# A gated cross-attention and MoLE feed-forward layer: the 26 last context rows in 32x32 tiles, and a new order around scores and values

## The reference, cut to what matters

```python
q = (layernorm(x) @ Wq.T + bq) * D ** -0.5      # x: (4, 1024, 256), 16 heads of D = 16
k, v = ctx @ Wk.T + bk, ctx @ Wv.T + bv         # ctx: (4, 154, 256)
k, q = xpos_apply(k, True), xpos_apply(q, False)        # rotation by position
attn = softmax(q @ k.T) @ v                     # per head, over the 154 context rows
x = x + tanh(g_xattn) * (attn @ Wo.T + bo)
h = relu(mole(layernorm(x), W1, b1, A1, B1, R1))        # 256 -> 1024, with 3 routed LoRA experts
x = x + tanh(g_ffn) * mole(h, W2, b2, A2, B2, R2)       # 1024 -> 256
```

## Time and profile before

| | us |
|---|---|
| median of 3 runs | 584.95 |
| lowest, highest | 583.15, 585.03 |
| the profiled execution, its own time | 584.23 |
| its span (first to last instruction) | 582.4 |
| TensorE busy in the span | 522.7 |
| VectorE busy | 402.3 |
| ScalarE busy | 245.5 |
| GpSimd busy | 84.8 |

### The profile page before, as it was taken

One profiled execution on the slowest core, in us unless ns is written; L12 is line 12 of the kernel. 1 busy time (PEld: TensorE's weight loads), 2 busy tenths in 40 slices (PEclk: granted clock), 3 DMA queues, 4 the chain that ended last, 5 costly groups with the idle time before them and its releaser, 6 DMA issues.

```text
span 582.4 us, 8570 instructions
## 1 busy us (share of the span) xinstructions
PE 522.7 (90%) x3384; PEld 399.7 (69%) x3384; DVE 402.3 (69%) x920; ACT 245.5 (42%) x405; POOL 84.8 (15%) x121
## 2 busy tenths in 40 slices
PE   2668865999999899999999899999999999999897
PEld 1545454864988488855987488856987498748687
DVE  4658465866889568958889478958888487925533
ACT  3152614364353616453364616454355526251330
POOL 2418012010020112011110112011100120010000
PEclk9965986999999999999999999999999999999898
DMA  8301010010100110010101010111002000100001
GB/s 273 98 21 37 1 37 2 0 51 1 37 1 38 37 38 2 38 49 0 38 1 57 19 37 2 38 48 32 7 1 75 0 1 2 41 35 1 1 36 37
DMA packets 6131, 18.49 MB, mean 32 GB/s; under 512 B 932, under 2 KB 1772, under 8 KB 5964
## 3 DMA queue, kind: packets, MB, share of 16 engines
q10 hardware_dynamic: 4005, 12.53, 6.2%
q1 hardware_dynamic: 2087, 5.42, 2.8%
HBM read 13.49 MB, written 4.19 MB: 30 GB/s over the span
## 4 chain that ended last, share of the span: by engine, by line
PE 68%; DVE 15%; ACT 10%; POOL 3%; issue 3%; DMA 1%; ACTq 0%; DVEq 0%; POOLq 0%
PE psF L1084 11%; PE psF L1145 10%; PE psX L1128 5%; DVE max_t L748 5%; PE psX L1199 4%; PE psX L995 4%; PE psX L1013 4%; ACT probs L536 4%; PE psO L1213 3%; ACT xn L426 3%; PE psF L1213 3%; PE psF L1216 3%; PE psO L1216 3%; PE psX L1115 3%; DVE ln_s L589 2%
## 5 line engine op out<-in xcount | busy, mean ns | idle before, releaser
L748 DVE TENSOR_REDUCE max_t<-psX 128x4 fp32r<-128x616 f32 x128 | 99.4, 795 | 5.1 <-PE psX L1128 2.1
L536 ACT ACTIVATE probs<-psX 128x1024 f32<-128x1024 f32 x64 | 64.0, 1024 | 50.9 <-PE psX L1199 50.9
L1145 PE MATMUL psF<-w_hi,h_hi 128*128 128x284 f32 (+1 forms) x240 | 72.7, 303 | 0.0
L1145 PE MATMUL psF<-w_lo,h_hi 128*128 128x284 f32 (+1 forms) x240 | 70.8, 295 | 0.0
L1145 PE MATMUL psF<-w_hi,h_lo 128*128 128x284 f32 (+1 forms) x240 | 70.7, 295 | 0.0
L1128 PE MATMUL psX<-km,qT 96*128 96x308 f32 x256 | 63.5, 335 | 5.7 <-DVE max_t L748 5.0
L1128 PEld LDWEIGHTS psX<-km,qT 96*128 96x128 f32 x256 | 47.9, 200 | 20.8 <-DVE max_t L748 12.4
L446 ACT ACTIVATE h_hi<-psF 128x512 fp32r<-128x512 f32 x59 | 34.4, 594 | 56.1 <-PE psF L1090 56.0
L326 POOL TENSOR_TENSOR x<-x,tab 128x256 f32<-128x256 f32 x32 | 22.3, 727 | 195.6 <-DMA x<-in_x_dram 195.6
L1145 PEld LDWEIGHTS psF<-w_hi,h_hi 128*128 128x128 f32 x240 | 45.7, 190 | 4.8 <-issue 4.6
L1084 PE MATMUL psF<-xT_lo,w_hi 128*128 128x512 f32 x118 | 47.0, 402 | 0.0
(11 more groups left out here) (187 smaller groups left out, 1044.2 us busy)
## 6 DMA issues: line engine op xcount, KB each, us to landing
x<-in_x_dram ACTq DMA_DIRECT2D x8, 512.0 KB, 3.4
x_ln<-in_x_dram ACTq DMA_DIRECT2D x7, 512.0 KB, 3.3
out_dram<-x ACTq DMA_DIRECT2D x7, 512.0 KB, 2.6
heads_t<-in_w_dram SPq DMA_DIRECT2D x1, 1024.0 KB, 8.2
heads_t<-in_w_dram SPq DMA_DIRECT2D x1, 994.0 KB, 4.8
tab<-in_tables_dram SPq DMA_DIRECT2D x1, 674.0 KB, 6.7
x_ln<-in_x_dram SPq DMA_DIRECT2D x1, 512.0 KB, 3.3
wkv_sb<-in_wkv_dram SPq DMA_DIRECT2D x1, 512.0 KB, 9.3
```

What stands on the lines that cost most here:

```text
L536: nc.scalar.activation(dst, psX[:, 2 * (i % 2):2 * (i % 2) + 2, :], ACT.Exp).then_inc(sc_exp.sem, 1)
L748: V.tensor_reduce(max_t[:, k, half, :].rearrange("p (h g) -> p g h", h=2)[:, 2 * j:2 * j + 2, :], psX[:, 2 * j:2 * j + 2, 0:2 * S].rearran ...
L1145: ins = mm(out_bank(d, k)[:, cs], a[:, m, tokens(k)], w[:, m, cs], start=m == 0 and i == 0, stop=m == HT - 1 and i == 2)
```

## The change

The rest of the values no longer runs as a 128x128 block-diagonal product. `vr_sb` shrinks to 32 columns, and each head's rest is a product of its own of 32 rows and 32 columns (`values_rest`); heads that sit on the same 32 rows of `probs_r` (j) write the same bank: `pv_bank(j)` is psO for even j and psF 2 for odd j. A half (`half`) covers two values of j, that is eight heads. The main values go by `part`: four parts of four heads each, in the two banks. The order of heads in `wo` on the host follows. In the score stage, the second "rest" becomes score 3 (it was 5), main pairs come in the order 0, 2, 4, 6, 1, 3, 5, 7, and the places on TensorE become: values part 0 after score 3; context transposes after score 5; values part 1, the first half of the rest and `project_k` after score 7; then scores 8 and 9, the second half of the rest, parts 2 and 3, and after all of them the queries. `rotate_keys` is cut in two: the biases (`keys_bias`) stay in the score stage, the rotation and splitting move to the head of the next step on VectorE. Keys are transposed after output tile 1 and not before output tile 0, and `project_v` stands between the two tiles. In the last step, output tiles 0, 1, 2 take the places of 2, 0, 1.

```diff
-        vr_sb = sb("vr_sb", [P, NQ, P])
+        vr_sb = sb("vr_sb", [P, NQ, 32])
-            return psF[:, g // 2, :] if g % 2 else psO[:, :]
+            return psF[:, 2, :] if j % 2 else psO[:, :]
@@ score order
-                if i % 5 == 0:
-                    pe.wait_ge(max_rows[i // 5].sem, max_rows[i // 5].at(c))
+                if i in (0, 3):
+                    pe.wait_ge(max_rows[i // 3].sem, max_rows[i // 3].at(c))
@@ values
-                mm(pv_bank(g), vr_sb[:, g, :], probs_r[:, g, :], start=True, stop=False)
-                for j in range(4):
-                    h = 4 * g + j
-                    ins = mm(pv_bank(g)[32 * j:32 * j + 32, :], v_sb[:, h, :], probs[:, h % 8, :], start=False, stop=True)
+                half = part // 2
+                for q in (2 * (part % 2), 2 * (part % 2) + 1):
+                    for j in (2 * half, 2 * half + 1):
+                        ins = mm(tile_of(j, q), v_sb[:, 4 * q + j, :], probs[:, 2 * q + j % 2, :],
+                                 start=half == 0, stop=half == 1)
+            def values_rest(c, half):
+                if half:
+                    pe.wait_ge(pv_t.sem, pv_t.at(c, 2))
+                for q in range(4):
+                    for j in (2 * half, 2 * half + 1):
+                        rows = slice(32 * j, 32 * j + 32)
+                        ins = mm(tile_of(j, q), vr_sb[rows, q, :], probs_r[rows, q, :], start=half == 1, stop=half == 0)
+                if not half:
+                    ins.then_inc(pv_ps.sem, 1)
@@ VectorE, end of a step
                 head_blocks(c, 1)
+                if u == 1 and not last:
+                    keys_bias(b + 1)
                 head_norm(c, 0)
                 head_back(c, 0)
-                if u == 1 and not last:
-                    rotate_keys(b + 1)
+                head_low(c, 0)
                 head_blocks(c, 2)
-                head_low(c, 0)
+                head_blocks(c, 3)
+                head_norm(c, 1)
+                head_back(c, 1)
+                head_low(c, 1)
                 if not last:
                     q_bias(c + 1)
@@ tables
-SCORE_STEPS = [("rest", 0), ("main", 0), ("main", 2), ("main", 4), ("main", 6),
-               ("rest", 2), ("main", 8), ("main", 10), ("main", 12), ("main", 14)]
+SCORE_STEPS = [("rest", 0), ("main", 0), ("main", 2), ("rest", 2), ("main", 4), ("main", 6),
+               ("main", 1), ("main", 3), ("main", 5), ("main", 7)]
```

More of the change, by code:

```diff
@@ L538, in step @@
                         xT_high(c + 1)
-                    if i == 4 and not last and u == 1:
+                    if i == 5 and not last and u == 1:
                         ctx_copy(b + 1)
@@ L759, in gates2 @@
             def gates2(d, pr):
-                dve.wait_ge(g2_c.sem, g2_c.at(d, 3 if d is LAST - 1 and pr == 0 else 2 * pr + 2))
+                dve.wait_ge(g2_c.sem, g2_c.at(d, 2 * pr + 2))
                 K = slice(2 * pr, 2 * pr + 2)
@@ L817, in step @@
                     q_bias(c)
[L818 to L822, removed]
+                    keys_bias(b)
+                if u == 0:
                     rotate_keys(b)
                 q_sine(c, u)
-                if not first:
-                    head_low(d, 1)
                 q_sum(c)
@@ L922, in _ @@
             gates2(e, 0)
+            copy_z2(e, 2)
             copy_z2(e, 3)
@@ L1198, in scores, with tile_of, values @@
                     else:
-                        ins = mm(o_ps, km[:, n // 2, j, 0:P], qT[:, n // 2, :], start=True, stop=True)
+                        ins = mm(o_ps, km[:, n, j, 0:P], qT[:, n, :], start=True, stop=True)
                 ins.then_inc(sc_ps.sem, 1)
-            def values(c, g, first, last):
-                pe.wait_ge(sc_exp.sem, sc_exp.at(c, PV_AFTER[g]))
-                if g == 0:
+            def tile_of(j, q):
+                col = (q + 2 * (j % 2)) % 4
+                return pv_bank(j)[32 * col:32 * col + 32, :]
+            def values(c, part, first):
+                pe.wait_ge(sc_exp.sem, sc_exp.at(c, (3, 6, 8, 10)[part]))
+                if part == 0:
                     pe.wait_ge(maxT_s[1].sem, maxT_s[1].at(c))
@@ L1226, in step @@
                     project_k(b)
-                if u == 0:
-                    if not first:
-                        pe.wait_ge(pv_t.sem, pv_t.at(d, 3))
                     key_transposes(b)
@@ L1295, in step @@
                         transpose_x(c + 1, psF, ln1_out, xT_ps)
-                    if i == 3 and u == 1 and not last:
+                    if i == 3:
+                        values(c, 0, first)
+                    if i == 5 and u == 1 and not last:
                         ctx_transposed(b + 1, ctx_sb)
-                    if i == 6 and u == 1 and not last:
-                        project_k(b + 1)
-                    if last and i in (1, 6, 9):
+                    if i == 7:
+                        values(c, 1, first)
+                        values_rest(c, 0)
+                        if u == 1 and not last:
+                            project_k(b + 1)
+                    if last and i in (1, 5, 9):
                         if i == 1:
@@ L1303, in step @@
                             pe.wait_ge(w1_lo_s.sem, w1_lo_s.at(d))
-                        out_tile(LAST - 1, 2, *{1: (0, 3), 6: (3, 5), 9: (5, 8)}[i])
-                    if i in PV_SLOT:
-                        values(c, PV_SLOT[i], first, last)
+                        out_tile(LAST - 1, 0, *{1: (0, 3), 5: (3, 5), 9: (5, 8)}[i])
+                values_rest(c, 1)
+                values(c, 2, first)
+                values(c, 3, first)
                 if not last:
@@ L1309, in step @@
                     project_q(c + 1, False)
-                values(c, 3, first, last)
             pe.wait_ge(const_v.sem, 1)
@@ L1411 @@
     wkv = _np.concatenate([i["L0_xattn_Wk"].T[:, perm], i["L0_xattn_Wv"].T], 1)
-    wo = i["L0_xattn_Wo"].T.reshape(2, 2, 4, D, E).transpose(2, 1, 3, 0, 4).reshape(P, -1)
+    heads = [4 * ((col + 2 * g) % 4) + 2 * f + g for col in range(4) for g in range(2) for f in range(2)]
+    wo = i["L0_xattn_Wo"].T.reshape(H, D, E)[heads].reshape(4, 2, 2, D, E).transpose(0, 1, 3, 2, 4).reshape(P, -1)
     w1 = i["L0_ffn_W1"].reshape(FT, P, HID).transpose(1, 0, 2).reshape(P, -1)
```

68 lines of the change are left out of this document (35 added, 33 removed).

## The result

| | before | after |
|---|---|---|
| median of 4 runs each, same chip | 584.05 us | 592.45 us |
| lowest and highest | 582.86 to 585.03 | 589.24 to 592.63 |
| ratio, 95% interval | | 1.0132 [1.009, 1.0174] |
| profiled execution, its span | 584.23, 582.4 | 592.31, 590.5 |
| mean granted clock in it | 0.953 | 0.944 |

The prediction said 580.3 us, with a range of 576.5 to 588.0. The time lies above the range and on the other side of no change.

The account below looks back on a forecast made before the run. TensorE, with 68% of the chain, was taken to bound the kernel, along with step heads hanging on VectorE. The terms -3.6 + 3.15 - 1.35 - 2.2 = -4.0 us took 584.23 to 580.3, range 576.5 to 588.

Parts of the forecast that it names:

- Part 1: Score stage: each half of the rest in 32x32 tiles takes TensorE 1.05 us, saving 2.1 us a step.
- Rival 2: In `values_rest`, row tiles take turns: a half costs 2.0 us, 15.2 us on top, 595.5 us; chance 0.13.
- Part 2: Score 3 waits for the maxima rows, 2.3 us after their DMA issue; this eats half the tiles' saving.
- Part 3: Score stage walked: T comes sooner by 0.95 us (step 2), 1.45 (step 3), 2.15 (step 0), 2.7 (last step).
- Part 4: VectorE's work at a step's head: bias ends at T + 3.1; statistics 0.45 us sooner or 1.05 later.
- T: Moment when the score stage's last group ends and output tiles begin, 210.2 us in step 2 before the change.
- u = 1: After steps 1, 3, 5: keys' rotation behind T makes the statistics 1.05 us later, three times, +3.15 us.
- u = 0: After steps 2, 4, 6: statistics about 0.45 us sooner, three times, -1.35 us.
- Step 0's head: After step 0: heads and bias done at 80.05 for 83.86, statistics about 86.2 for 89.80, -3.6 us.
- rival 3: At step 1's head the clock may stay at 2.4 GHz, up to 3 us more, 577.5 us; chance 0.12.
- the end: After the last step: `project_out` starts at 530.2 for 532.43, -2.2 us.
- Rival 1: The middle eats the gain: rows 0.3 us later or VectorE's line 0.5 longer; 582 to 586 us, chance 0.17.

Follow-up runs that it names:

- e7: Changed kernel with the second row of maxima used one score later: 589.17 us, ratio 1.0111.
- e1: Changed kernel with GpSimd's cosine product cut to two heads of one token tile in every step but the first: 576.87 us, ratio 0.9894.
- e2: Kernel before, with GpSimd's cosine waiting until VectorE has turned the second half of the heads back: 592.67 us, ratio 1.0166.
- e8: Changed kernel; after u = 1 the cosine runs beside the values' bias, sine and sum behind the statistics; after u = 0 cosine on VectorE: 595.0 us.
- e12: Changed kernel with GpSimd's cosine cut into four instructions, one for each token tile: 596.33 us in one run.
- e6: Changed kernel with the cosine on VectorE ahead of the sine, none on GpSimd: 588.13 us, median of nine, ratio 1.003.
- e11: Changed kernel with cosine on VectorE, second maxima row one score later, half of output tile 2 ahead of the routes' transposes: 581.11 us, ratio 0.9967.
- e9: Changed kernel with the edits of e8 and e7 together: 591.02 us, ratio 1.0125.
- e5: Changed kernel with half of output tile 2 ahead of the routes' transposes on TensorE: 588.43 us, ratio 1.0121.

## Why the prediction was wrong, point by point

- **Part 1, the rest at 1.05 us a half: right.** 1.02 measured (the prediction's other estimate was 1.03), and two row groups that write psO and psF 2 cost nothing more. Rival 2 (row tiles take turns, 2.0) is out. The row that 1.05 leans on, L1034, has 16 instructions of 256 columns, not 512; it serves because its four tiles stream 1024 columns each, as those of L1216 do, and as the tiles of a half now do in 1.02 us.
- **Part 2, the rows: right in kind, 0.3 us short.** TensorE waits 1.41 to 1.47 us for them in steps 2 to 6 (forecast 1) and starts score 3 at 2.59 after the issue, for the forecast 2.3; the 0.15 for the semaphore stood on no row. e7 prices the wait at 0.7 to 1.0 us a step.
- **Part 3, stage lengths: right.** 190.70 to 210.39 is 19.7 us (forecast 19.6) and 252.55 to 273.84 is 21.3 (21.2). The 0.3 of part 2 hardly shows in them.
- **Part 4, the failed step.** "Sine 1.3" and "T + 3.1 + 3.5" for the rotation took VectorE's durations from rows in which GpSimd was idle, though the same part had just moved GpSimd's cosine to T + 3.1, exactly onto them. I used the cosine's row for its start and not for what would run beside it. The price: after u = 1 the statistics start at T + 18.07 for 16.1, three times 2.0; after u = 0 at T + 11.51 for 10.75, three times 0.8. The second is less than 2.2, because I had put the queries' sum at T + 6.9, where the terms I gave add up to 3.1 + 1.3 + 1.15 = 5.6; that error of 1.3 hid a part.
- **Step 0's head: right, without rival 3.** TensorE's idle time before `project_out` fell from 4.71 to 2.91 us, and it starts at 80.23 (forecast 80.05), the statistics at 86.50 (86.2). But the clock did not stay up: it was at the 1.2 GHz level for 3.4 us from 80.4 and for 13.7 from 87.2, together as long as before (6.8 and 10.2).
- **The clock** was thought of at the start only (rival 3). TensorE's idle time after u = 1 was forecast at 1.9 us and came to 3.8, and behind it the clock fell in the middle: 0.9 us after each u = 1. It fell once more in step 4's score stage, behind the wait for the rows (1.2 us).
- **The account.** 3 x 1.9 (measured +3.0 for +1.05) + 2 x 0.9 + 2.1 (after u = 0, one with the clock's 1.2) + 3 x 0.9 (clock) + 0.9 (step 0) - 1.0 (the end) = 12.2 us. Forecast -4.0, measured +8.1 in the profiled executions: 12.1 apart.
- **The rest of the sum came out in sign, but not in size.** e1, where only the collision is missing, lies 8.4 us under before in the profiled runs, for the sum's -4.0: step 0 and what follows it at -5.3 (forecast -3.6), the end at -4.7 (-2.2), u = 0 at -0.96 each (-0.45) and u = 1 at +0.86 each (+1.05); half clock behind two waits takes 1.85 back. Part of the excess at both ends is the clock's: before has 17 us at the 1.2 GHz level between 80 and 103 us and 6.8 between 545 and 575, e1 has 10.2 and, up to its last 2 us, none.
- **The rivals** had no such mechanism. Rival 1 named the right place ("VectorE's line at the head of a batch is 0.5 longer"), at a quarter of the size, and the slower side was given to the tiles alone. Its other clause, rows 0.3 us later than put, came true and cost next to nothing. The stated condition for a wrong forecast, statistics after u = 1 over 1.5 us later than put, is what happened (2.0).

The Trainium skill, "SBUF — State Buffer", section "Who interferes with whom", says that VectorE and GpSimd share a port pair with an exclusive lock: an instruction of VectorE with two inputs in SBUF contends with one of GpSimd that reads SBUF, and the one issued first holds the lock for the whole instruction. The traces agree: 3.6 for 1.39 us beside the cosine in e2, no change for the bias with one input in e8, turns by the instruction in e12. Read beside the move of the queries, that section would have been a term of the sum.

## What to carry to other kernels

When an edit moves one engine's instruction in time, list what will then run beside it on the others, GpSimd beside VectorE above all, and don't take durations from rows where the neighbour was idle. On an engine whose line is full to the next due result, standing still, idle time and more work cost the same, so judge a repair by when the last of its line starts (T + 15.97, 18.07), not by whether one row recovered. A free neighbour engine isn't free if it stops yours: 1.23 us more on VectorE beat 2.4 on GpSimd.

## What the runs showed of the hardware that I had not expected

- GpSimd's cosine and VectorE's sine hardly overlap: four sines of 1.39 us in sum take 3.60 to 3.63 beside a cosine of 2.4 (one after the other would be 3.8), and the cosine itself 2.6 to 2.75 in the changed kernel.
- The same kernel, e6, gave 580.7 and 588.7 us, with mean granted clocks of 0.957 and 0.938. In the middle of the kernels, stretches at half clock, from 3.4 us to 13.7 (17.1 once, in e12), mostly began at or right behind waits of TensorE of 1.4 to 3.8 us, and other waits of the same length had none behind them. Some began where TensorE had no wait over 0.7 us ahead of them (e11 at 454.4, e9 at 203.7). Removing one such wait (e5) kept the clock at one place; what decides it elsewhere stays open.
